# Graph network layer: a fifth PSUM bank for gather-by-matmul, small sums moved into shared banks, partition-split transfers

## The reference, cut to what matters

```python
h = maximum(layernorm(x), 0)                       # 12500 nodes x 16
for i in range(3):
    W   = (edge_attr @ ew[i] + eb[i]).reshape(400000, 16, 16)
    msg = einsum('ei,eio->eo', h[src], W)          # 400000 edges, sorted by dst
    h   = segment_sum(msg, dst, 12500) + h @ rw[i] + rb[i]
    if i < 2: h = relu(batchnorm(h))
out = x + relu(h) @ pred_w + pred_b
```

## Time and profile before

| | us |
|---|---|
| median of 3 runs | 7210.68 (7210.26 to 7211.35) |
| the profiled execution, its own time | 7214.45 |
| its span, first to last instruction | 7212.7 |
| PE busy | 6865.8 (95%) |
| DVE busy | 6331.5 (88%) |
| POOL busy | 5236.5 (73%) |
| ACT busy | 5078.0 (70%) |

### The profile page before, as it was taken

The page is one execution under the profiler, slowest core; times in us unless marked ns, Lnnn a source line. Parts: engine busy times, 40 slices in busy tenths (PEclk is TensorE's granted clock), DMA queues, the critical chain, the costliest instruction groups (busy, mean ns, idle before and its releaser), DMA issues.

```text
span 7212.7 us, 132587 instructions
## 1 busy us (share of the span) xinstructions
PE 6865.8 (95%) x49944; PEld 5867.0 (81%) x49944; DVE 6331.5 (88%) x7670; ACT 5078.0 (70%) x8348; POOL 5236.5 (73%) x5543
## 2 busy tenths in 40 slices
PE   5999999999999899999999999999999999999998
PEld 3888888888888788888888888878888888888887
DVE  6888888888888888888888888888888888888888
ACT  4777777777777577777777777757777777777775
POOL 4777777777777377777777777747777777777775
PEclk7999999999999899999999999989999999999999
DMA  6111111111111111111111111111111111111111
GB/s 47 33 32 31 31 32 33 31 32 32 33 33 30 30 31 33 32 33 31 31 33 33 33 30 33 33 31 31 32 30 32 33 33 32 30 32 33 32 30 29
DMA packets 712195, 231.96 MB, mean 32 GB/s; under 512 B 571634, under 2 KB 662682, under 8 KB 711557
## 3 DMA queue, kind: packets, MB, share of 16 engines
q1 hardware_dynamic: 494193, 175.68, 10.9%
q0 software_dynamic: 177024, 45.67, 6.4%
q10 hardware_dynamic: 40340, 2.11, 0.7%
HBM read 219.48 MB, written 3.55 MB: 31 GB/s over the span
## 4 chain that ended last, share of the span: by engine, by line
PE 63%; DVE 30%; issue 6%; DVEq 1%; ACT 0%; DMA 0%; ACTq 0%; SPq 0%
PE bank L1236 50%; DVE xg L821 11%; DVE xbig L760 8%; PE bank L1203 7%; DVE spread L816 6%; PE bank L1246 1%; DVE agg L862 1%; PE bank L1245 1%; DVE merge L848 1%; DVE rows_room L752 1%; PE bank L1267 1%; PE bank L1269 1%; PE bank L1311 1%; PE bank L1189 1%; DVE mask L799 0%
## 5 line engine op out<-in xcount | busy, mean ns | idle before, releaser
L569 POOL DMA_INDIRECT xg<-node_table,idx x5532 | 5233.0, 946 | 1922.7 <-issue 1749.8
L1236 PE MATMUL bank<-nodes,low_hot 128*128 128x448 f32 x26901 | 5795.0, 371 | 233.7 <-DVE spread L816 201.9
L1236 PEld LDWEIGHTS bank<-nodes,low_hot 128*128 128x128 f32 x26901 | 4970.1, 188 | 914.3 <-DVE spread L816 335.6
L816 DVE TENSOR_TENSOR spread<-mask,bank 128x448 f32<-128x448 uint8 x3843 | 2207.8, 613 | 712.2 <-PE bank L1236 703.1
L1076 ACT ACTIVATE low_hot<-distance,one 128x640 fp32r<-128x640 bf16 (+1 forms) x3000 | 2278.2, 832 | 531.7 <-PE bank L1236 531.5
L1068 ACT ACTIVATE distance<-key_all,low_id 128x640 bf16<-128x640 int16 (+1 forms) x3000 | 2275.7, 829 | 66.9 <-ACT low_hot L1076 66.9
L821 DVE TENSOR_REDUCE xg<-spread 128x80 f32<-128x2240 f32 (+1 forms) x750 | 1907.9, 2544 | 25.7
L760 DVE TENSOR_TENSOR xbig<-xg,bank 128x1280 f32<-128x1280 f32 (+1 forms) x750 | 1356.4, 1809 | 0.5 <-issue 0.3
L1033 ACT ACTIVATE z<-bank 128x144 f32<-128x144 f32 x471 | 136.9, 291 | 1324.2 <-PE bank L1203 1324.2
L1203 PE MATMUL bank<-xbig,rows_room 128*32 128x144 f32 x12450 | 571.0, 290 | 4.2 <-DVE xbig L760 4.2
L1203 PEld LDWEIGHTS bank<-xbig,rows_room 128*32 128x32 f32 x12450 | 458.9, 110 | 83.1 <-issue 81.0
(11 more groups left out here) (121 smaller groups left out, 1242.5 us busy)
## 6 DMA issues: line engine op xcount, KB each, us to landing
key_all<-edge_keys SPq DMA_DIRECT2D x282, 320.0 KB, 3.6
xg<-node_table,idx POOLq DMA_INDIRECT x5532
ea<-in_edge_attr SPq DMA_DIRECT2D x375, 100.0 KB
key_all<-edge_keys SPq DMA_DIRECT2D x93, 352.0 KB, 3.6
idx<-in_src SPq DMA_DIRECT2D x375, 7.5 KB
xbig<-node_table SPq DMA_DIRECT2D x3, 672.0 KB
xbig<-in_src ACTq DMA_DIRECT2D x1, 937.5 KB
node_table<-rows_room SPq DMA_DIRECT2D x2, 468.8 KB
```

Source lines behind the costliest of these rows:

```text
L569: pool.indirect_dma_start(out=xg[u][:, j, :], out_offset=None, in_=table[:, :], in_offset=bass.IndirectOffsetOnAxis(ap=idx[u][:, j:j + 1], ...
L816: nc.vector.tensor_tensor(spread[:, t - t0, :, :], mask[k % PAIR][:, t, :].unsqueeze(1).to_broadcast([P, D, FINE]), p_sel[n % BANKS].rearr ...
L1236: last = nc.tensor.matmul(p_sel[place_in_all % BANKS], low_hot[:, i // 2, t, :], nodes[:, i, :, :].rearrange("p d f -> p (d f)"), start=i ...
```

## The change

The picks get a fifth bank (2 to 6). The transposed sums and the message sums leave bank 2 and go to columns 144 and up of banks 0 and 1, beside the sums of the rounds. So a round's sums wait for the copy of the transposed sums two rounds earlier and, from the second round of a quad on, for the adds of the quad before; the transposes lose their waits for `s_zT` and `s_add`. ACT waits for each transposed round by itself. The three table parts of layers 1 and 2 and the four parts of the result are each issued as two DMAs, over 120 and over 5 partitions.

```diff
-BANKS = 4
+BANKS = 5
...
-        p_zT = [bank[2][:, i * 2 * SPAN:i * 2 * SPAN + SPAN] for i in range(PAIR)]
-        p_zxT = [bank[2][0:D, i * 2 * SPAN + SPAN:(i + 1) * 2 * SPAN] for i in range(PAIR)]
-        p_agg = [bank[2][q % GANG * WIN:q % GANG * WIN + D, q // GANG * SPAN:(q // GANG + 1) * SPAN]
-                 for q in range(QROUNDS)]
+        SIDE = D + FD
+        p_zT = [bank[i][:, SIDE:SIDE + SPAN] for i in range(PAIR)]
+        p_zxT = [bank[i][0:D, SIDE + SPAN:SIDE + 2 * SPAN] for i in range(PAIR)]
+        p_agg = [[bank[i][q % GANG * WIN:q % GANG * WIN + D, SIDE + q // GANG * SPAN:SIDE + (q // GANG + 1) * SPAN]
+                  for q in range(QROUNDS)] for i in range(PAIR)]
...
-        p_sel = [bank[3 + i][:, 0:SELW] for i in range(BANKS)]
+        p_sel = [bank[2 + i][:, 0:SELW] for i in range(BANKS)]
...
-            return 2 * 16 + layer * (len(PARTS_OF_ROWS) - 1) * 16
+            return 2 * 16 + layer * (len(PARTS_OF_ROWS) - 1) * 2 * 16
...
+        def side_of(q):
+
+            return ((q + 1) * QROUNDS + 1) % PAIR
...
-                        sp.dma_start(by_node[:, here, :], rows[:, here, :]).then_inc(s_table, 16)
+                        for some in slice(0, SPREAD_P), slice(SPREAD_P, NODE_P):
+                            sp.dma_start(by_node[some, here, :], rows[some, here, :]).then_inc(s_table, 16)
...
-                sp.dma_start(out.rearrange("(p m) d -> p m d", m=PER)[:, here, :], rows[:, here, :]).then_inc(s_out, 16)
+                for some in slice(0, SPREAD_P), slice(SPREAD_P, NODE_P):
+                    sp.dma_start(out.rearrange("(p m) d -> p m d", m=PER)[some, here, :], rows[some, here, :]
+                                 ).then_inc(s_out, 16)
...
-                    nc.vector.tensor_tensor(here, here, p_agg[r % QROUNDS], ALU.add).then_inc(s_add, 1)
+                    nc.vector.tensor_tensor(here, here, p_agg[side_of(q)][r % QROUNDS], ALU.add).then_inc(s_add, 1)
...
-                if rounds:
-                    act.wait_ge(s_T, layer * R + rounds[-1] + 1)
                 for r in rounds:
                     n = layer * R + r
+                    act.wait_ge(s_T, n + 1)
...
                 if n >= PAIR:
                     pe.wait_ge(s_z, n - PAIR + 1)
+                    pe.wait_ge(s_zT, n - PAIR + 1)
+                if r > QROUNDS:
+                    pe.wait_ge(s_add, layer * R + (r - 1) // QROUNDS * QROUNDS + CREDIT)
...
                 if rounds:
-                    n, after = layer * R + rounds[0], layer * R + rounds[-1] + 1
-                    pe.wait_ge(s_z, after)
-                    if n:
-                        pe.wait_ge(s_zT, n)
-                    pe.wait_ge(s_add, layer * R + rounds[-1] - rounds[-1] % QROUNDS + CREDIT)
+                    pe.wait_ge(s_z, layer * R + rounds[-1] + 1)
...
+                side = side_of(q)
...
-                        nc.tensor.matmul(p_agg[q], w_now[:], zT[:, q, :], start=True, stop=False)
+                        nc.tensor.matmul(p_agg[side][q], w_now[:], zT[:, q, :], start=True, stop=False)
```

More of the change, by code:

```diff
@@ L250, in gnn_kernel @@
         p_z = [bank[i][:, 0:D + FD] for i in range(PAIR)]
-        p_zT = [bank[2][:, i * 2 * SPAN:i * 2 * SPAN + SPAN] for i in range(PAIR)]
-        p_zxT = [bank[2][0:D, i * 2 * SPAN + SPAN:(i + 1) * 2 * SPAN] for i in range(PAIR)]
-        assert PAIR * 2 * SPAN <= 512
-        p_agg = [bank[2][q % GANG * WIN:q % GANG * WIN + D, q // GANG * SPAN:(q // GANG + 1) * SPAN]
-                 for q in range(QROUNDS)]
+        SIDE = D + FD
+        assert SIDE + 2 * SPAN <= 512
+        p_zT = [bank[i][:, SIDE:SIDE + SPAN] for i in range(PAIR)]
+        p_zxT = [bank[i][0:D, SIDE + SPAN:SIDE + 2 * SPAN] for i in range(PAIR)]
+        p_agg = [[bank[i][q % GANG * WIN:q % GANG * WIN + D, SIDE + q // GANG * SPAN:SIDE + (q // GANG + 1) * SPAN]
+                  for q in range(QROUNDS)] for i in range(PAIR)]
         p_far, p_far_agg = bank[0][0:FAR_WIN, 0:D + FD], bank[1][0:D, 0:FAR_WIN]
         p_farT, p_farxT = bank[2][:, 0:FAR_WIN], bank[2][0:D, FAR_WIN:2 * FAR_WIN]
-        p_sel = [bank[3 + i][:, 0:SELW] for i in range(BANKS)]
+        p_sel = [bank[2 + i][:, 0:SELW] for i in range(BANKS)]
         p_t = [bank[i][0:NODE_P, 0:SUB * D].rearrange("p (m d) -> p m d", d=D) for i in range(TURNS)]
@@ L533, in _ @@
                 here = slice(ENDS[k] * SUB, ENDS[k + 1] * SUB)
-                sp.dma_start(out.rearrange("(p m) d -> p m d", m=PER)[:, here, :], rows[:, here, :]).then_inc(s_out, 16)
-            sp.wait_ge(s_out, (len(ENDS) - 1) * 16)
+                for some in slice(0, SPREAD_P), slice(SPREAD_P, NODE_P):
+                    sp.dma_start(out.rearrange("(p m) d -> p m d", m=PER)[some, here, :], rows[some, here, :]
+                                 ).then_inc(s_out, 16)
+            sp.wait_ge(s_out, (len(ENDS) - 1) * 2 * 16)
         @block.gpsimd
@@ L1035, in copy_transposed @@
             def copy_transposed(layer, rounds):
-                if rounds:
-                    act.wait_ge(s_T, layer * R + rounds[-1] + 1)
                 for r in rounds:
                     n = layer * R + r
+                    act.wait_ge(s_T, n + 1)
                     if r % QROUNDS == 0 and n:
                         act.wait_ge(s_mm, layer * QUADS + r // QROUNDS)
-                    nc.scalar.activation(zT[:, r % QROUNDS, :], p_zT[n % PAIR], ACT.Copy)
-                    nc.scalar.activation(zxT[:, r % QROUNDS, :], p_zxT[n % PAIR], ACT.Copy).then_inc(s_zT, 1)
+                    nc.scalar.activation(zT[:, r % QROUNDS, :], p_zT[r % PAIR], ACT.Copy)
+                    nc.scalar.activation(zxT[:, r % QROUNDS, :], p_zxT[r % PAIR], ACT.Copy).then_inc(s_zT, 1)
             def copy_segments_far(layer):
@@ L1244, in transpose_round @@
                 pe.wait_ge(s_merge, n + 1)
-                nc.tensor.matmul(p_zT[n % PAIR], z[r % PAIR][:, D:D + FD], merge[r % SHIFTS][:], start=True, stop=True)
-                nc.tensor.matmul(p_zxT[n % PAIR], z[r % PAIR][:, 0:D], merge[r % SHIFTS][:], start=True, stop=True).then_inc(s_T, 1)
+                nc.tensor.matmul(p_zT[r % PAIR], z[r % PAIR][:, D:D + FD], merge[r % SHIFTS][:], start=True, stop=True)
+                nc.tensor.matmul(p_zxT[r % PAIR], z[r % PAIR][:, 0:D], merge[r % SHIFTS][:], start=True, stop=True).then_inc(s_T, 1)
             def transpose_rounds(layer, rounds):
                 if rounds:
-                    n, after = layer * R + rounds[0], layer * R + rounds[-1] + 1
-                    pe.wait_ge(s_z, after)
-                    if n:
-                        pe.wait_ge(s_zT, n)
-                    pe.wait_ge(s_add, layer * R + rounds[-1] - rounds[-1] % QROUNDS + CREDIT)
+                    pe.wait_ge(s_z, layer * R + rounds[-1] + 1)
                 for r in rounds:
@@ L1266, in messages_of @@
                     for q in some:
-                        nc.tensor.matmul(p_agg[q], w_now[:], zT[:, q, :], start=True, stop=False)
+                        nc.tensor.matmul(p_agg[side][q], w_now[:], zT[:, q, :], start=True, stop=False)
                     for q in some:
-                        last = nc.tensor.matmul(p_agg[q], eb_now[:], zxT[:, q, :], start=False, stop=True)
+                        last = nc.tensor.matmul(p_agg[side][q], eb_now[:], zxT[:, q, :], start=False, stop=True)
                 last.then_inc(s_mm, 1)
```

## The result

| | before | after |
|---|---|---|
| median, us | 7210.94 (7210.26 to 7211.35, 4 runs) | 7114.01 (7112.25 to 7125.27, 4 runs) |
| ratio, 95% interval | | 0.987 (0.9856 to 0.9884) |
| span of the profiled execution | 7212.7 | 7123.5 |

What follows compares the result with a forecast made beforehand. PE, handed to and fro with DVE, was taken as the bound, with POOL's gathers at the same pace limiting any gain. 88.6 + 3.1 + 8.6 + 0.7 = 101.0 us off gave 7109.7 by the median, range 7096 to 7132.

Steps and rivals of the forecast that it cites:

- The fifth bank takes the stalls: PE's picks: nearly all 201.9 us of waits for DVE's banks go, with restarts some 260 us by PE alone.
- The gathers allow 88.6 us: Layer ends: distance from last gather to last sums falls from 52.8, 24.0 and 25.0 to 4.4 us each.
- The index waits of layer 0, 3.1 us: POOL's small waits for indices loaded behind the products vanish once DVE's products come earlier; bounds 0 and 4 us.
- The moved sums at nothing: Rounds' sums now wait for earlier transposed copies and adds; the extra waits before 471 rounds were costed at 0.
- The bound of 141 us: Upper cost of the added waits before 471 rounds, at POOL's 0.30 between two instructions, in PE's time.
- The table and the result, 9.3 us: Split writes: POOL starts layers 1 and 2 4.3 us earlier each, 8.6 us; the result's end gives 0.7 us.
- When the gathers bind, ACT's order brings a new wait, at no cost: ACT's copy of fetched rows precedes key work, delaying `low_hot`, picks and messages; costed at nothing, as self-correcting.
- 1 (PE gains less: Rival, 12%: with half of the 0.54 us a group, layer 0 shrinks by 34 us, not 51.5; 7127 us.
- 4 (the wait only moves): Rival, 3%: PE's wait moves from the bank to `low_hot`, so no change; 7210 us.
- 2 (the gathers are not the bound): Rival, 4%: POOL's 0.30 us between gathers shrinks and PE shows all its gain; 6942 us.
- 3: Rival, 4%: PE's clock falls at the new wait before each quad's messages, making the kernel slower; 7281 us.
- a sign that I would be wrong: The granted clock dipping within layers, named beforehand as what would show the slower, fallen-clock rival.

Runs made afterwards that it cites:

- few_gathers_before: The kernel before with two gathers left out in each group from the sixth of a layer on; 7210.37 us, ratio 1.0.
- one_more_pick_before: The kernel before with 16 more tiles a layer picked by PE in place of gathered by POOL; 7303.35 us, ratio 1.013.
- place_only: The changed kernel with four banks for the picks in place of five, moved sums and split transfers kept; 7207.58 us, ratio 0.9997.
- split_only: The kernel before with only the table and result transfers divided into 120 + 5 partitions; 7207.92 us, ratio 0.9997.
- bank_only: The changed kernel with transfers over 125 partitions in one DMA as before, fifth bank and moved sums kept; 7122.42 us.
- changed_again: The changed kernel run once more, unaltered, for a second profile; 7114.39 us, ratio 0.9869.
- act_order: The changed kernel with ACT's copy of the fetched rows moved behind the first half of the key work; 7115.43 us, ratio 0.9864.
- few_gathers_after: The changed kernel with two gathers left out in each group from the sixth of a layer on; 6911.71 us, ratio 0.9587.
- one_more_pick_in_8: The changed kernel with 16 more tiles a layer picked by PE in place of gathered by POOL; 7063.87 us, ratio 0.9798.
- pick21: The changed kernel with 21 more tiles a layer picked in place of gathered; 7045.83 us, ratio 0.9767.
- pick32: The changed kernel with 32 more tiles a layer picked in place of gathered; 7048.26 us, ratio 0.9772.

## Why the prediction was right, step by step

- **PE and DVE at the bank, POOL beside them at the same pace.** Shown: few_gathers_before changes nothing, one_more_pick_before costs 93 us, place_only brings the 200.6 us of waiting back.
- **The fifth bank takes the stalls.** Shown, and the size by PE alone was too small: 260 forecast (201.9 and the restarts), 296 measured against place_only. The group's idle row does not hold all that a stall costs; where the other 36 us lay is open. That it made no difference to the forecast is luck of a kind: the gathers allow less, so any size over some 100 us would have done. The lead shows the same pace. From the last gather of a group to ACT's copy of its rows it is 48 to 53 us all through layer 0 in the kernel before; in the first profile of the changed kernel it is 49.6, 33.5, 17.3 and 2.2 at groups 3, 21, 41 and 61, and from there on never over 4.1. That is 0.82 us a group, where 0.54 was taken from the idle time alone.
- **The gathers allow 88.6 us.** By the first profile the distances fell from 52.8, 24.0 and 25.0 to 5.1 each, 86.5 us; the distance was put at 4.4. From the last gather's issue to DVE's start it took 2.27 where at most 1.98 were taken (that was the time to the end of the DMA traffic, and the reader starts later), and the sums started 0.65 after the multiply (2388.02 + 2.15 to 2390.82) where 0.26 were taken. Together 0.7 us a layer. The second part is the new wait and the low clock, which do show here. PE's messages stand before the last sums and waited for ACT's copies; these are their first and last matmuls, in the changed kernel and in the one before:

```profile
2389.01 0.54 PE L1274 MATMUL bank<-zT,w_now 128*16 128x100 f32 x8 [9.90 <-ACT zxT L1051]
...
2390.39 0.51 PE L1276 MATMUL bank<-zxT,eb_now 16*16 16x100 f32 x2
```

```profile
2435.84 0.36 PE L1267 MATMUL bank<-zT,w_now 128*16 128x100 f32 x8 [0.73 <-ACT zxT L1044]
...
2436.70 0.34 PE L1269 MATMUL bank<-zxT,eb_now 16*16 16x100 f32 x2
```

After 9.90 us of standing the granted clock was 0.50 from 2389.0 to 2390.8, and the messages took 1.8 us and ended after DVE's multiply; at 1.00 they had taken 1.2, which here would have ended with it. This is an estimate of 0.4 us a layer for the low clock; no run takes it away.
- **The index waits of layer 0, 3.1 us.** They are gone, but the reason given was not needed. In split_only, where PE is as slow as before, the same stretch of layer 0 (1000 to 2390 us) has no such wait either, by POOL's waits:

```profile
POOL xg L572 <- DMA ea<-in_edge_attr: 6.1, 20, 0.3
```

These are twenty gaps of 0.3, the ordinary ones, where the earlier trace rows had 26 with 8.5 us and up to 0.9. place_only has the same twenty. What had caused the longer ones in the profiled execution of before is open.
- **The moved sums at nothing.** Shown with four banks by place_only beside split_only, 0.3 us apart. The bound of 141 us was far off. No row or run here shows two engines colliding in a bank.
- **The table and the result, 9.3 us.** 8.0 by the medians of bank_only and changed_again, 9.3 by the three places on the timeline (4.3, 4.05 and 0.95). The start of the gathers moves in both kernels and counts only where they bind.
- **When the gathers bind, ACT's order brings a new wait, at no cost.** Shown inside the layers by act_order; at their ends it is part of the 0.7 us above. I had named two places, `low_hot` and the messages; it came at the messages.
- **Rivals.** 1 (PE gains too little) is excluded by few_gathers_after, 4 (the wait only moves) too. 2 (the gathers are not the bound) is excluded by the same run and by one_more_pick_in_8; the gaps between gathers stayed 0.30. 3 is half true: the clock does fall inside layers, which I had named as a sign that I would be wrong, and it does not make the kernel slower. The sign was badly chosen: it tells that PE waits, not that the wait costs time. That one fall is made up before the next is my reading; no run shows it by itself.

The sum, 101.0, was worked out on the span of one execution. Between spans of one gather step, before and changed_again, it is 101.1 (7212.7 to 7111.6), and that is nearer than the terms deserve: by the timelines the layers' ends give 86.3 of 88.6, layer 0's gathers 3.5 of 3.1, the way from the last sums of a layer to the next layer's gathers 9.8 of 8.6, and the end 1.5 of 0.7. The small misses cancel, by luck. By the medians it is 96.9 in the first comparison and 96.0 in the second (7210.37 to 7114.39), because the profiled execution of before lay 3.77 above its median.

## What to carry to other kernels

When an engine looks like the bound, ask what second chain runs beside it at nearly the same pace and how large its lead is: what the first engine gains is worth only what that lead allows, here 96 of 299 us. An engine that issues DMAs can be full at 74% busy; divide its stretch by its count of instructions, not its busy time by the span. After such a change the costs swap sides, so edits tried before it (an earlier start of the gathers, another share of work between two engines) must be weighed again: the same edit of the transfers went from no measurable difference to 8 us, and one more pick in eight groups from +93 to -50 us.

## What the runs showed of the hardware that was not expected

- **The gather's step varies between executions,** by 2.5 ns in 1.25 us: 2308.49 us for 1843 steps in the first profile and 2303.97 in changed_again, of the same kernel. Over 5532 gathers this is 13.5 us, and a kernel bound by gathers shows it in its time: that first execution took 7125.27 and the other three 7112.25 to 7114.47. act_order repeats it, with 2307.81 us in layer 1 of the profiled execution, which took 7125.16, and 7113.61 to 7116.08 in the others. It is not the chip: pick21 ran on the same one as act_order, and its step is 1.2503 (2277.96 us for 1822). A kernel that PE binds shows no such spread: pick32 had the longer step in its profiled execution, 1.2521 (2267.57 us for 1811), and its four runs lie within 3.3 us. What causes it is open.
- **The granted clock fell after a wait of 2.06 us and small matmuls behind it,** within a layer that is otherwise dense, where in the kernel before, with stalls of up to 1.0 us, it stood at 1.00 throughout the layers. It was back in the next stretch shown. Not every such wait brings it down: PE waited 65 times before the messages in that profile, and the clock fell 29 times inside the layers.
